# Head attention: value products as 64x64 tiles with 32 moving columns

## The reference, cut to what matters

```python
NUM_HEADS, HEAD_DIM = 16, 64
qkv = (x @ w_qkv + b_qkv).reshape(B, L, NUM_HEADS, 3 * HEAD_DIM)
q, k, v = jnp.split(qkv, 3, axis=-1)
k = k + pos_enc[None, :, None, :]
attn = softmax(einsum('blhd,blgd->blhg', q, k) / 8)      # 16 x 16 for each token
out = einsum('blhg,blgd->blhd', attn, v)                 # the products changed here
return out.reshape(B, L, 1024) @ w_out + b_out
```

## Time and profile before

| | us |
|---|---|
| median of 3 runs | 1093.25 (1093.06 to 1094.26) |
| the profiled execution, its own time | 1093.4 |
| its span in the trace | 1091.2 |
| TensorE busy in the span | 1078.2 |
| GpSimd busy | 796.1 |
| VectorE busy | 797.2 |
| ScalarE busy | 590.6 |
| values of head attention (line 704) | 41.2 to 199.2, 1024 records |

### The profile page before, as it was taken

How to read it: one execution, slowest core, us unless ns; L and a number is a source line. 1 busy time by engine, 2 the same in 40 slices (tenths; PEclk the granted TensorE clock), 3 DMA queues, 4 the chain that set the end, 5 groups by cost and what they waited for, 6 DMA issues and landing times.

```text
span 1091.2 us, 22061 instructions
## 1 busy us (share of the span) xinstructions
PE 1078.2 (99%) x8783; PEld 685.0 (63%) x8783; DVE 797.2 (73%) x1247; ACT 590.6 (54%) x939; POOL 796.1 (73%) x524
## 2 busy tenths in 40 slices
PE   9999999999999999999999999999999999999998
PEld 7898998877745455455455455455455545467886
DVE  4658866476675877877877878878878877895553
ACT  4634453576665555555555555655655655654442
POOL 5789998644467899898898899899899898950000
PEclk9999999999999999999999999999999999999999
DMA  7323333200000000200000000000000000000000
GB/s 257 129 79 99 114 103 99 78 1 1 1 1 2 1 1 2 105 4 1 1 1 1 2 1 2 1 1 2 1 1 2 1 2 1 2 0 11 11 1 20
DMA packets 26870, 31.10 MB, mean 28 GB/s; under 512 B 3345, under 2 KB 23185, under 8 KB 25489
## 3 DMA queue, kind: packets, MB, share of 16 engines
q1 hardware_dynamic: 26448, 29.69, 8.1%
q10 hardware_dynamic: 320, 0.01, 0.0%
HBM read 20.12 MB, written 9.44 MB: 27 GB/s over the span
## 4 chain that ended last, share of the span: by engine, by line
PE 90%; DVE 5%; POOL 2%; ACT 2%; issue 1%; SPq 0%; DMA 0%; DVEq 0%; POOLq 0%; ACTq 0%
PE o_ps L1722 21%; PE mx_ps L1675 7%; PE st_ps L1694 5%; PE st_ps L1700 5%; PE st_ps L1697 5%; PE ha_banks L651 4%; PE bank L2127 3%; PE bank L2129 3%; PE bank L2128 3%; PE mx_ps L1613 3%; PE pj_ps L1627 3%; PE pj_ps L1619 2%; PE ha_banks L704 2%; PE ha_banks L715 2%; PE mx_ps L1607 2%
## 5 line engine op out<-in xcount | busy, mean ns | idle before, releaser
L2040 POOL TENSOR_TENSOR acc<-acc,prob 128x1024 f32<-128x1024 f32 x192 | 468.6, 2441 | 49.0 <-ACT prob L1867 38.8
L1867 ACT ACTIVATE prob<-st_ps 128x1024 f32<-128x1024 f32 x256 | 248.6, 1023 | 197.7 <-PE st_ps L1706 104.0
L1722 PE MATMUL o_ps<-prob,v_cur 128*64 128x512 f32 x1024 | 246.4, 602 | 0.0
L1930 DVE TENSOR_REDUCE mx_part<-mx_ps 128x1 f32<-128x512 f32 x258 | 164.8, 666 | 58.0 <-PE mx_ps L1675 58.0
L1933 DVE TENSOR_REDUCE mx_part<-mx_ps 128x2 f32<-128x1024 f32 x78 | 93.6, 1200 | 62.0 <-PE mx_ps L1675 62.0
L1722 PEld LDWEIGHTS o_ps<-prob,v_cur 128*64 128x64 f32 x1024 | 63.8, 136 | 108.9 <-issue 72.8
L1955 DVE RECIPROCAL rden<-rden 128x128 f32<-128x128 f32 x128 | 119.5, 934 | 0.0
L1675 PEld LDWEIGHTS mx_ps<-k_hi,q_hi 64*128 64x128 f32 x414 | 46.5, 183 | 106.7 <-issue 72.6
L1675 PE MATMUL mx_ps<-k_hi,q_hi 64*128 64x512 f32 x414 | 111.9, 457 | 1.2 <-DVE mx_part L1933 0.6
L2040 POOL TENSOR_TENSOR acc<-prob 128x1024 f32<-128x1024 f32 x32 | 76.7, 2397 | 33.9 <-ACT prob L1867 33.3
L1700 PE MATMUL st_ps<-q_hi,d_lo 64*128 64x512 f32 x512 | 100.9, 390 | 0.0
(11 more groups left out here) (414 smaller groups left out, 2266.2 us busy)
## 6 DMA issues: line engine op xcount, KB each, us to landing
v_rows<-ha_v SPq DMA_DIRECT2D x8, 1024.0 KB, 4.1
ha_vt<-v_rows SPq DMA_DIRECT2D x16, 512.0 KB, 4.0
q_max<-mx_turned SPq DMA_DIRECT2D x128, 1.0 KB
h_w<-in_h SPq DMA_DIRECT2D x2, 1024.0 KB, 8.0
w_raw<-in_w SPq DMA_DIRECT2D x8, 192.0 KB, 3.4
head_wkv<-in_wkv SPq DMA_DIRECT2D x2, 512.0 KB, 5.8
m_w<-in_m SPq DMA_DIRECT2D x3, 256.0 KB, 2.9
out<-fin SPq DMA_DIRECT2D x3, 256.0 KB, 2.2
```

Source lines behind the costliest of these rows:

```text
L1722: mm = pe.matmul(o_ps[rows(h), :], v_cur[:, m % 2, j, rows(h)], prob[:, (16 * m + slot) % RING, h, :], start=(j == 0), stop=(j == KT - 1), ...
L1867: act.activation(prob[:, n % RING, :, :], st_ps[:, slot % 2, :, :], ACT.Exp, scale=SCALE).then_inc(s_exp, 1)
L1930: dve.reduce_max(mx_part[:, h, i, keys:keys + 1], maxima_banks(q, n)[h], AX_X).then_inc(s_mxr, 1)
L2040: pool.tensor_tensor(total, old, new, ALU.add).then_inc(s_acc, 1)
```

## The change

The contraction over 128 rows is split into two of 64. Rows 0 to 63 hold groups 0 to 3 and rows 64 to 127 hold groups 4 to 7, so each half needs 4 groups of columns: `wide`, `own` and the products are 32 columns wide (8 heads x 4 groups), and there are 64 products in a turn. The four of one (t, sequence) lie on the four 64x64 quarters of the array: `rows(odd)` chooses the output partitions, `rows(low)` the rows. The lower half writes bank 6 and the upper one bank 7, for all 8 places t; half r of the turn is the half t of both banks, and `y_ps` lies in the second half of bank 7. The waits follow: half 0 waits for both copies and y of the turn before, half 1 waits until half 0 has been copied, `f.tensor` and the experts' first down product wait for the copy of half 1 too. In the last turn the expert weights' product is moved between the two halves.

```diff
         else:
-            pe.wait_ge(s_oc, 2 * (i - 2) + 1)
+            pe.wait_ge(s_oc, 2 * (i - 2) + 2)
...
+    HALF = GROUPS // 2
...
-    own = room.sb("own", [P, GROUPS])
+    own = room.sb("own", [P, HALF])
...
-    wide = [room.sb(f"wide{i}", [P, SEQS, G // 2, HEADS, GROUPS]) for i in range(2)]
+    wide = [room.sb(f"wide{i}", [P, SEQS, G // 2, HEADS, HALF]) for i in range(2)]
...
-    o = room.sb("o", [P, G, SEQS, PAIRS, GROUPS])
+    o = room.sb("o", [P, G, SEQS, 2, PAIRS, HALF])
...
-    o_ps = [banks[:, n, :].rearrange("r (t s n) -> r t s n", s=SEQS, n=TURN) for n in (6, 7)]
-    y_ps = o_ps[1][:, 0, :, :]
+    o_ps = banks[:, 6:8, :].rearrange("r l (t s n) -> r l t s n", s=SEQS, n=TURN // 2)
+    y_ps = banks[:, 7, CH // 2:CH // 2 + SEQS * TURN]
...
             if n >= 1 and r == 0:
-                pe.wait_ge(s_oc, 2 * (n - 1) + 1)
+                pe.wait_ge(s_oc, 2 * (n - 1) + 2)
+                pe.wait_ge(s_yc, n)
+            if r == 1:
+                pe.wait_ge(s_oc, 2 * n + 1)
             if r == 0:
 
                 f.bank_free(pe, n + 1)
-            if n >= 1 and r == 1:
-                pe.wait_ge(s_yc, n)
...
                 for odd in range(2):
-                    mm = pe.matmul(o_ps[r][rows(odd), t, seq, :], vt[n % 2][:, r * G // 2 + t, rows(seq)],
-                                   wide[r][:, seq, t, PAIRS * odd:PAIRS * odd + PAIRS, :],
-                                   start=True, stop=True, skip_group_check=True)
+                    for low in range(2):
+                        mm = pe.matmul(o_ps[rows(odd), low, r * G // 2 + t, seq, :],
+                                       vt[n % 2][rows(low), r * G // 2 + t, rows(seq)],
+                                       wide[r][rows(low), seq, t, PAIRS * odd:PAIRS * odd + PAIRS, :],
+                                       start=True, stop=True, skip_group_check=True)
...
         act.wait_ge(s_o, 2 * n + r + 1)
-        act.activation(o[:, r * G // 2:r * G // 2 + G // 2, :, :, :].rearrange("r t s p g -> r (t s p g)"),
-                       o_ps[r][:, :, :, :].rearrange("r t s n -> r (t s n)"), ACT.Copy).then_inc(s_oc, 1)
+        of = slice(r * G // 2, r * G // 2 + G // 2)
+        act.activation(o[:, of, :, :, :, :].rearrange("r t s l p g -> r l (t s) (p g)"),
+                       o_ps[:, :, of, :, :].rearrange("r l t s n -> r l (t s) n"), ACT.Copy).then_inc(s_oc, 1)
...
             if t == 0:
-                pe.wait_ge(head.s_oc, 2 * head.TURNS - 1)
+                pe.wait_ge(head.s_oc, 2 * head.TURNS)
...
                 head.tensor_outs(pe, TURNS - 1, 0)
+                e.tensor_weights(pe, 2)
                 head.tensor_outs(pe, TURNS - 1, 1)
-                e.tensor_weights(pe, 2)
                 e.tensor_down(pe, 2)
```

More of the change, by code:

```diff
@@ L691, in tensor_out @@
             if n >= 1 and r == 0:
-                pe.wait_ge(s_oc, 2 * (n - 1) + 1)
+                pe.wait_ge(s_oc, 2 * (n - 1) + 2)
+                pe.wait_ge(s_yc, n)
+            if r == 1:
+                pe.wait_ge(s_oc, 2 * n + 1)
             if r == 0:
                 f.bank_free(pe, n + 1)
-            if n >= 1 and r == 1:
-                pe.wait_ge(s_yc, n)
-            if n == 0 and r == 1:
+            if n == 0 and r == 0:
                 pe.wait_ge(f.s_cen, CHUNKS)
@@ L714, in tensor_y @@
         for p in range(PAIRS):
-            mm = pe.matmul(y_ps, w.wo[:, p, :], o[:, :, :, p, :], start=p == 0, stop=p == PAIRS - 1)
+            mm = pe.matmul(y_ps, w.wo[:, p, :], o[:, :, :, :, p, :].rearrange("r t s l g -> r (t s) l g"), start=p == 0, stop=p == PAIRS - 1)
         mm.then_inc(s_y, 1)
@@ L798, in vector_masks @@
                               0.0, None, ALU.is_ge)
-        dve.tensor_scalar(own[:, :], w.mask_g[:, 0:P:HEADS], 0.0, None, ALU.is_ge).then_inc(s_same, 1)
+        for low in range(2):
+            of = slice(HD * low, HD * low + HD, HEADS)
+            d = dve.tensor_scalar(own[rows(low), :], w.mask_g[rows(low), of], 0.0, None, ALU.is_ge)
+        d.then_inc(s_same, 1)
     def vector_begin(dve):
@@ L920, in scalar_y @@
         act.activation(tokens[:, :, n // 2, n % 2, :, :].rearrange("r s g t -> r t s g"),
-                       y_ps.rearrange("r s n -> r (s n)").rearrange("r (t s g) -> r t s g", s=SEQS, t=G),
+                       y_ps.rearrange("r (t s g) -> r t s g", s=SEQS, t=G),
                        ACT.Copy).then_inc(s_yc, 1)
@@ L959, in gpsimd_wide @@
             d = pool.tensor_tensor(wide[r][:, seq, :, :, :],
-                                   t.unsqueeze(3).to_broadcast([P, G // 2, HEADS, GROUPS]),
-                                   own[:, :].unsqueeze(1).unsqueeze(1).to_broadcast([P, G // 2, HEADS, GROUPS]), ALU.mult)
+                                   t.unsqueeze(3).to_broadcast([P, G // 2, HEADS, HALF]),
+                                   own[:, :].unsqueeze(1).unsqueeze(1).to_broadcast([P, G // 2, HEADS, HALF]), ALU.mult)
         d.then_inc(s_wide, 1)
```

## The result

The kernel after takes 1100.98 us, the median of 4 runs (1100.87 to 1105.38), against 1093.76 before: a ratio of 1.0076, 95% interval 1.005 to 1.0102. It is slower by 7.2 us, where the prediction said 8.4 more than the profiled execution, 1101.7. The same kernel once more on another chip: 1101.60 (5 runs, 1101.20 to 1103.21), ratio 1.0074 (1.0061 to 1.0086).

The account below looks back on a forecast made before the run. TensorE was taken to bound the kernel, its time counting one for one. Shape changes 6.7 + 0.9, last turns 1.7, GpSimd's relief -0.9 gave +8.4: 1101.8 from the profiled 1093.4, 1101.7 against the median; range 1094.5 to 1106.

Parts of the forecast that it names:

- -0.9: Odd turns' key projections: lighter GpSimd work lets ScalarE's query copies go sooner, removing TensorE's stops; 0.9 us less.
- a set of four: Four value products side by side on the array's quarters: taken as 62 ns, bound by the 64-column weight load.
- +0.02 us a piece: Value products: 32 sets a turn at 62 ns against 32 pairs at 61 ns, so no gain.
- way out: Value products, leaving their tile shape for another: 0.10 us each time.
- 24 x 0.28: Four value pieces in each of six odd turns, each entered and left between key projections: +6.7 us.
- The way in: Change from 128x64 projections into 64x64 values: taken as 0.10 us, bounds 0 and 0.15, not shown in the trace.
- The even turns: Last value piece before 128x64 query projections in six even turns: 6 x 0.15 = +0.9 us.
- Half 1's wait for half 0: Middle turns, waiting for half 0's copy: nothing, unless the copy slows by over 0.2 us.
- +1.7: Last turns, where copy waits have no cover: 0.5 - 0.6 + 0.5 + 1.4, less 0.1 for the shorter `wide`.
- packing pays: Rival, value products: the stream sets the set of four at 31 ns; result -7.5, 1086 us; chance 0.12.
- changes are nearly free: Rival, borders between 64x64 and 128x64 shapes: free or hidden, leaving +1.3, 1094.6 us; chance 0.08.
- a floor of 25 ns: Rival, value products: each of 2048 records costs at least 25 ns, +20 on top, 1122 us; chance 0.03.

Follow-up runs that it names:

- e5: Kernel before, with GpSimd spreading out only 4 of the 8 groups from turn 1 on, all else unchanged: 1091.72 us, ratio 0.9984.
- e2: Kernel before, with the value products of odd turns in two pieces in place of four: 1092.12 us, ratio 0.9988.
- e4: Kernel after, with each value product moving 16 of its 32 columns: 1103.60 us in one execution, with 6.8 us at half clock.
- e6: Kernel before, with each value product moving 32 of its 64 columns, shape 128x64 kept: 1093.35 us in one execution.
- e8: Kernel after, with each value product loading 32 of its 64 columns of values, 32 moving columns kept: 1089.64 us in one execution.
- e1: Kernel after, with the value products of odd turns in two pieces of 64 records in place of four of 32: 1099.21 us, ratio to before 1.0053.
- e3: Kernel after, first half of values directly behind the scores, second half behind projection units up to the third: 1105.90 us; same order on kernel before: 1104.28.
- e7: Kernel after, order scores, first half of values, two projection units, second half, other four units; ScalarE copies first half ahead of query copies: 1106.22 us, ratio 1.0114.
- e10: Kernel after, with 64 already satisfied semaphore waits put into TensorE's program at the start: 1105.17 us, ratio 1.0106.

## Why the prediction was right

**The bound.** TensorE led before and leads after, and what is added to it comes out at the end: the rest of the kernel takes 886.2 before and 886.3 after.

**GpSimd.** Two `wide` instructions take 1.18 to 1.20 us, as said; the page has

```profile
L967 POOL TENSOR_TENSOR ha_wide<-ha_pt,ha_own 128x256 f32<-128x256 f32 x64 | 38.2, 618 | 17.5 <-ACT ha_pt L923 16.0
```

against 1185 ns. The key projection's wait for ScalarE has vanished, as said: in the first piece of that odd turn after has 0.60 to the next start where the earlier trace rows has 0.96. The term was -0.9; e5 shows -0.74 in the middle turns by itself, in turns 5 and 9 alone, and after has more. Four pieces of the new shapes add 1.13 to an odd turn, the six turns 6.8; the turns show 1.01 in four, 0.68 in turn 9 and 0.59 in turn 5 without its stop, together 5.3. So 1.5 was absorbed: the 0.75 of turns 5 and 9 that e5 shows too, and 0.12 in every odd turn, where the first quarter took 0.53 and the projection behind it 0.93 before, against 0.46 and 0.88 further on. e5 has these 0.12 unchanged, so GpSimd's relief does not give them, and e2, whose key projection comes later, lacks them: they are covered by the time that the shapes take. The term was sized too small, and half of it has another reason than the one given.

**The products.** 60 to 61 ns a set of four: right. +0.02 us a piece was said; a quarter has 0.03 more than its way out, a half in an even turn 0.02 less than before. e4 and e6 show that the stream is not the reason, and e8 that the columns of the weights are; that the load is the reason stays argued, as said there.

**The changes of shape.** 24 x 0.28: the pair of a piece and a projection takes 1.62 against 1.34, to the hundredth what was said. The way in, the one term without a row, shows in the projection of 1.02 in place of 0.87: 0.10 of it is the way in, 0.05 the slower start. The even turns cost 0.09 to 0.14 and not 0.15, and only five of the six lie between y0 and y11: 0.6 in place of 0.9. The middle turns: said 6.7 + 0.9 - 0.9 = 6.7, measured 6.8 + 0.6 - 1.5 + 0.77 for the stop = 6.67. That the two agree to 0.03 is luck: 0.6 more absorbed and 0.3 less in even turns stand against 0.77 of a stop that I did not foresee.

**The waits.** Half 1's wait for half 0 is hidden in every middle turn. In the last turns each wait came where it was said: `f.tensor` (0.35 idle, start 0.5 late), y (0.58), half 1 (0.42) and down (0.71). One was not said: turn 14's first half waits 0.35 for y's copy too, where before it had stood idle for 0.93 already, so it cost nothing. By turns: +0.49 (said 0.5), -0.69 (-0.6), -0.15 and +2.24 (1.9, less 0.1). Said +1.7, measured +1.90. No run takes these waits out by themselves; for the last turns the reason rests on the rows.

**The total.** 8.4 was said; 8.6 less 0.5 of an earlier start is what the trace has, 7.2 and 7.5 what the medians of the two sets have. What the half-clock stretches took in the first set's profile was in no term.

The rivals: packing pays, refuted by e4; changes are nearly free, refuted by the rows and e1; a floor of 25 ns, refuted by e8's 9 ns.

TensorE: Matmul & The Clock Gate in the Trainium skill, section "Wait — 56ns, not 53.3ns?", has start to start never below about 25 ns. For small tiles side by side this trace disagrees, with 15 ns a record (61 ns a set of four) and 9 ns in e8. The warning in TensorEngine Tiling (Array Packing) of the Trainium skill, section Instruction Overhead, against a factor from a dimension that is already small agrees with e4 and e6 in its effect, though e8 shows the weights' columns as what the time goes with.

## What to carry to other kernels

Before splitting a product over more tiles of the array, compare its moving columns with the columns of its weights. Here, in float32 with 64 columns of weights, products of 64, 32 and 16 moving columns cost the same time each, and the split doubles their number; four side by side then take what two took. Look at what stands next to them: here each border between tile shapes costs 0.10 us, and up to 0.06 more behind it, so a shape that differs from its neighbours pays at every interleaving. A new order that saves such borders has to be checked against the other engines' copies: e3 and e7 moved products together and spent most or half of the gain on new waits. And a change that helps an engine off the path (here 36 us of GpSimd) is worth what TensorE waited for it, 1.4 us in e5.

## What the runs showed that was not expected

- TensorE can run out of instructions. With twice as many small products it stopped once in after, which cost 0.77 us, and in e7 for up to 1.7 at a time. The stops of 0.4 us and more, in any of the runs, ended 2.3 to 2.8 us after the start of a 16 KB load of instructions (102.0 and 104.6; 132.3 and 135.0; 171.1 and 173.7; e10: 124.3 and 126.85), always at one place of the 256 instructions of a load, and waits put in at the start moved them to other products. Small changes of a kernel can so move its time by a microsecond or more without any other reason.
- The granted clock fell to half for 3.4 us after a stretch in which TensorE's records lay end to end (36.0 to 39.3), in one of the two executions of that kernel that were traced and not in the other; e3 on the kernel before has such a stretch at 39.8 too. What decides this is open.
